# A six-stage transformer kernel on one core: DVE's program without engine loops, its waits on constants, and without three semaphore increments

## The reference

```
x = x + 0.5 * _L0_ffn_ref(_layernorm(x), ...)     # stage 0: 128 -> 64, relu over 16 inner units, 64 -> 128
x = x + _L0_attn_ref(_layernorm(x), ...)          # stage 1: window attention, 16 heads, LN on q and k
x = x + 0.5 * _L0_ffn_ref(_layernorm(x), ...)     # stage 2: as stage 0
x = x + 0.5 * _L1_ffn_ref(_layernorm(x), ...)     # stage 3: product keys
x = x + _L1_attn_ref(_layernorm(x), ...)          # stage 4: attention of the top 51 queries of each head
x = x + 0.5 * _L1_ffn_ref(_layernorm(x), ...)     # stage 5: as stage 3
```

```
s, i = jax.lax.top_k(sim, k)
all_scores = (sx[..., :, None] + sy[..., None, :]).reshape(b, n, h, k * k)
scores, pk = jax.lax.top_k(all_scores, k)
o = jnp.einsum('bnd,bnhkd->bnhk', inputs, w_down)
o = jax.nn.gelu(o, approximate=False) * jax.nn.softmax(scores, axis=-1)
return jnp.einsum('bnhk,bnhkd->bnd', o, w_up)
```

## Time and profile before

| | us |
|---|---|
| median of 3 runs (1404.76 to 1406.58) | 1404.99 |
| the profiled execution: time / span | 1402.47 / 1400.3 |
| busy: PE / DVE / ACT / POOL | 1151.0 / 1115.1 / 914.3 / 721.3 |
| stage 0 (its prep to 28.4; FFN to 94.9) | 94.9 |
| stages 1 / 2, with their preps | 217.0 / 69.4 |
| prep of stage 3; stage 3 to the last product-key result | 21.3; 381.9 |
| stage 4, with its prep | 212.0 |
| prep of stage 5; stage 5 | 21.5; 382.3 |
| bout_bc's DMA: issue to landing | 3.0 |

### The profile page before, as it was taken

One profiled execution on the slowest core, in us unless ns is written; L12 is line 12 of the kernel. 1 busy time (PEld: TensorE's weight loads), 2 busy tenths in 40 slices (PEclk: granted clock), 3 DMA queues, 4 the chain that ended last, 5 costly groups with the idle time before them and its releaser, 6 DMA issues.

```text
span 1400.3 us, 58159 instructions
## 1 busy us (share of the span) xinstructions
PE 1151.0 (82%) x22892; PEld 944.9 (67%) x22892; DVE 1115.1 (80%) x3996; ACT 914.3 (65%) x2135; POOL 721.3 (52%) x645
## 2 busy tenths in 40 slices
PE   1773898976758899999999769999568999999986
PEld 1562666655727788888888447777447888888886
DVE  4873888867879899989995468888598889998980
ACT  1772566647657778787785426666558787787871
POOL 3315444514037778777775410000157778787772
PEclk9886999988959999999999979999769999999998
DMA  6000000000002222222222000000012222222222
GB/s 160 17 0 1 1 0 0 0 2 0 1 0 48 47 45 53 52 45 45 45 45 63 1 1 1 0 0 1 0 22 54 49 45 45 45 60 45 45 62 77
DMA packets 27519, 42.91 MB, mean 31 GB/s; under 512 B 6960, under 2 KB 18480, under 8 KB 27440
## 3 DMA queue, kind: packets, MB, share of 16 engines
q1 hardware_dynamic: 27440, 41.82, 13.5%
HBM read 6.15 MB, written 2.10 MB: 6 GB/s over the span
## 4 chain that ended last, share of the span: by engine, by line
PE 42%; DVE 23%; ACT 11%; issue 11%; POOL 6%; DMA 3%; SPq 2%; DVEq 1%; POOLq 0%; ACTq 0%
PE bank L1763 11%; DVE work L909 5%; POOL work L346 5%; ACT work L1075 4%; DVE work L952 4%; PE bank L1745 4%; DMA rowsD<-work 3%; PE bank L1471 3%; ACT L1234 2%; PE bank L1647 2%; SPq L316 2%; DVE bank L934 2%; PE bank L1484 2%; PE bank L1629 2%; PE bank L1736 2%
## 5 line engine op out<-in xcount | busy, mean ns | idle before, releaser
L1763 PEld LDWEIGHTS bank<-rowsD,work 128*32 128x32 f32 x16384 | 359.5, 194 | 91.8 <-issue 91.2
L1763 PE MATMUL bank<-rowsD,work 128*32 128x32 f32 x16384 | 370.3, 275 | 56.4 <-DMA rowsD<-work 37.3
L421 POOL TENSOR_SCALAR work<-work 128x1024 f32<-128x1024 f32 x64 | 185.2, 2894 | 135.1 <-ACT work L1239 135.1
L408 POOL TENSOR_TENSOR work<-work 128x512 f32<-128x512 f32 x128 | 161.3, 1283 | 40.2 <-ACT work L1267 28.6
L1267 ACT ACTIVATE work<-bank 128x512 f32<-128x512 f32 x128 | 74.8, 610 | 152.0 <-PE bank L1763 148.8
L1239 ACT ACTIVATE work<-work 128x128 f32<-128x128 f32 x512 | 161.0, 404 | 4.1 <-DVE work L972 4.1
L1248 ACT ACTIVATE work<-work 128x128 f32<-128x128 f32 x512 | 160.2, 409 | 0.0
L423 POOL TENSOR_TENSOR work<-work 128x1024 f32<-128x1024 f32 x64 | 157.2, 2456 | 5.3
L952 DVE STREAM_TRANSPOSE work<-work 128x1024 f32<-128x1024 f32 x128 | 151.2, 1219 | 0.0
L453 POOL TENSOR_SCALAR xn<-x_sb,negmean,rstd 128x128 f32<-128x128 f32 x48 | 25.8, 539 | 207.9 <-DVE shift L562 179.6
L1774 PE MATMUL bank<-kout,work 128*128 128x128 f32 x1024 | 128.1, 278 | 3.0 <-POOL work L408 3.0
(11 more groups left out here) (193 smaller groups left out, 2315.7 us busy)
## 6 DMA issues: line engine op xcount, KB each, us to landing
rowsD<-work SPq DMA_DIRECT2D x256, 128.0 KB, 2.4
x_sb<-in_L_attn_x_dram SPq DMA_DIRECT2D x8, 256.0 KB, 4.7
out_dram<-x_sb SPq DMA_DIRECT2D x4, 512.0 KB, 5.3
headsel<-in_c_headsel_dram SPq DMA_DIRECT2D x1, 512.0 KB, 5.4
work<-in_L_ffn_key_in_dram SPq DMA_DIRECT2D x1, 512.0 KB, 8.0
kout<-in_L_ffn_key_out_dram SPq DMA_DIRECT2D x4, 128.0 KB, 4.3
work<-in_L_ffn_keys_dram SPq DMA_DIRECT2D x1, 256.0 KB, 2.9
wqkv<-in_L_attn_W_qkv_dram SPq DMA_DIRECT2D x1, 192.0 KB, 5.3
```

Of the source, the lines that this page charges most:

```text
L408: last = nc.gpsimd.tensor_tensor(cg[:, par, :].rearrange("p (j t) -> p j t", j=NCH)[:, :, half * 64:half * 64 + 64], csb[:, par, 512 * hal ...
L421: nc.gpsimd.tensor_scalar(wmask, both, 1.0 - 5e-7, None, ALU.is_ge).then_inc(s["wm"], 1)
L1763: last = nc.tensor.matmul(bank[2 + half][k * NK:(k + 1) * NK, :] .rearrange("p (j t c) -> p t c j", j=NCH, t=16)[:, t % 16, :, :], xrows[: ...
```

## The change

All of DVE's engine loops become Python loops, so the program holds every iteration with constant waits and addresses. The three `dve.sem_inc(s_go, 1)` are left out. Other engines keep their programs. Lines below L533 move up by one, those below L907 by two and those below L932 by three.

```diff
             def statistics(first, count, s, updated):
 
                 dve.wait_ge(s["x"], updated)
-                dve.sem_inc(s_go, 1)
                 for t in range(count):
...
                 if k == 0:
                     dve.wait_ge(s_x, 16 * NG)
-                    with dve.Fori(0, NT) as n:
+                    for n in range(0, NT):
                         nc.vector.bn_stats(stats[:, bass.ds(n, 1), :], x_sb[:, bass.ds(n, 1), :]).then_inc(s["stat"], 1)
...
-                    with dve.Fori(0, NG // 2 - 1) as i:
+                    for i in range(0, NG // 2 - 1):
                         sums(2 * i + 1, 1)
                         update(2 * i, 0)
...
-                with dve.Fori(0, NP_ // 2 - 2) as i:
+                for i in range(0, NP_ // 2 - 2):
                     sequence(2 * i + 1, 1)
                     sequence(2 * i + 2, 0)
...
                     dve.wait_ge(s["sim"], base + n + 1)
-                    dve.sem_inc(s_go, 1)
                     for c in range(2 * PH):
...
                     dve.wait_ge(s["cand"], base + n + 1)
-                    dve.sem_inc(s_go, 1)
                     for h in range(PH):
...
-                with dve.Fori(1, NPAIR - 1) as p:
+                for p in range(1, NPAIR - 1):
                     tile(2 * p, 0)
                     tile(2 * p + 1, 1)
```

## The result

The changed kernel took 1384.66 us (median of 4 runs, 1382.69 to 1385.71) against 1404.9 us before (median of 4, 1404.76 to 1406.58): ratio 0.9854, 95% interval 0.9841 to 0.9866. That is 1.5% less time, clear of the noise though smaller than 2%. The forecast was 1383.4 us. The profiled execution took 1384.7 us (span 1382.8) where that of before took 1402.47 (span 1400.3).

The account below looks back on a forecast made before the run. No engine's total decides: DVE alone paces stage 0's statistics, ACT leads the FFN, and a closed ring of waits paces stages 3 and 5. Terms summed to 21.6 us, taking 1404.99 to 1383.4; range 1375 to 1394.5.

Parts of the forecast that it names:

- the ring: Stages 3 and 5: DVE, SyncE's rowsD DMA, PE and ACT wait in a closed circle, 22.14 and 21.71 us a pair.
- (a): Stage 0's loop of 32 statistics: each goes from 0.492 to 0.197 us, saving 9.3 us (8.9 to 9.5).
- (b): Stage 0's FFN loop: DVE gains 0.5 us per pair of groups, but ACT leads; saving 0.7 us (0 to 1.9).
- the halving: Stage 0's FFN: of DVE's gain, 1.5 to 1.9 us, less than half was counted, 0.7 us, since ACT leads.
- (c): Increments of s_go, about 0.11 us each where DVE sets the time: 0.8 us in stage 2, 0.3 at stage ends.
- (d): Stage 3, inside the ring: 0.44 us a pair over 14 pairs, 6.2 us (3.5 to 9.1), plus 0.4 at its start.
- the piece set aside as plus or minus 0.2: L913 inside the ring, 0.60 to 0.86 us long: shifting it may give or take 0.2 us a pair, 2.8 a stage.
- (g): Longer program, DVE's listed instructions 1291 to 3986: at most 52 more instruction packets, hidden if fetched ahead, cost 0.
- (e): Stage 5, without statistics: 0.25 us a pair over 14 pairs, 3.5 us (1.4 to 6.3), plus 0.4 at its start.
- (f): Stages 1 and 4: DVE is on neither chain, so 0 (0 to 0.5, counted in the stage ends).
- fetches show: Rival: 21 to 52 new fetches each stall DVE 1.87 us inside the ring; 1423 us at the low end, chance 0.05.
- the two losses named there: Stage 3's lower bound, 0.25 us a pair: 0.15 us stay before L535, and L985 gains nothing.

Follow-up runs that it names:

- the product-key run: Kernel before with only DVE's product-key loop unrolled and the two increments of its front left out: 1397.44 us, ratio 0.9954.
- the statistics loop alone: Kernel before with one edit, stage 0's loop over 32 statistics unrolled: 1391.63 us, ratio 0.9909.
- either pad: Changed kernel plus one extra DVE reciprocal per product-key tile pair: in even tiles (inside the ring) 1387.43 us, in odd tiles (outside it) 1385.46 us.

## Why the prediction was right, and which terms were off

The forecast of 1383.4 us and its range held, and of the steps the largest two, the statistics loop and the ring, were right in mechanism. Several sizes were off, and partly cancelled.

- **(a) The statistics loop**, 9.3 us: 9.24 us measured from the first statistic to PE, in the changed kernel and alone. The price per instruction was exact; x landed 0.27 us sooner besides.
- **(b) Stage 0's FFN**, 0.7 us (0 to 1.9): 1.7 us measured. DVE's own gain, 0.5 us in a pair of groups, was sized rightly (11.16 to 10.64). The step that failed is the halving, "DVE can only give back the lag with which it ends behind ACT". A group went from 5.58 to 5.32 us. ACT's eight blocks, 0.66 us apart, need 5.3 us, so both engines were within 0.3 us of each other, and the chain by line named one of them.
- **(c) The increments**, 0.11 us each: 0.110 by the product-key run, 0.11 by the group of stage 0, and nothing for the one in front of L909. In stage 2, 0.8 us were forecast and 0.2 came: most groups fell by 0.11 us, but in one DVE now waits 0.46 us for ACT.
- **(d) Stage 3**, 0.44 us a pair: 0.31, stage and prep 4.6 us against 6.6. L978 to L909 gave 0.39 where 0.33 was forecast. The second part, 0.12 from L909 to L934, came to nothing, because L911 became longer in the odd tiles (0.63 to 0.78 us in the rows of one pair, median of all 0.64 to 0.77). That was the piece set aside as plus or minus 0.2. The rest is (g).
- **(e) Stage 5**, 0.25 us a pair: 0.19; by the medians of the pairs (21.73 to 21.46) it is 0.27. L978 to L909 gave 0.18 and L909 to L934 0.13, together 0.31, and SP to PE took 0.12 back, which is the fetches of (g).
- **(f) Stages 1 and 4**, 0: right as a mechanism. The +1.7 us of stage 1 is the granted clock, which the repeated run shows (217.3 us with nothing changed) and the line through all twelve traces. Stage 4's -0.9 was +0.7 in the repeated run.
- **(g) A longer program**, 0: this is the term that was wrong in kind. The instruction queue brought 23 packets more, within the 52 allowed for. DVE itself never stood still for a fetch: its only two issue idles after, 0.2 us each, at L682 and L735, were there before (L683, L736). But a fetch that falls into the transfer to rowsD delays it, and PE waits for that transfer in the ring. The rival "fetches show" looked for the cost on DVE and was off there; its path was the DMA. It cost 0.6 us in one pair of stage 3 (22.38 against 21.75) and 0.75 and 0.6 in two of stage 5 (22.21 and 22.06 against 21.45), 2.0 us together.

  Over the ring's eleven pairs per stage, the kernels with DVE's loop (before, the statistics loop alone) have no such fetch and no pair more than 0.3 us above the median. The seven runs with it unrolled and the transposes in their old place (six programs) have two or three such pairs each, 18 in all, and each of the 18 has a fetch 2.6 to 3.4 us behind the issue of its transfer. The sixteen from 3.2 us on cost 0.40 to 0.86 us, the four at 2.6 us (two of them not among the 18) 0.18 to 0.39. Fetches in the half microsecond before the issue, and at 1.9 and 4.4 us behind it, cost nothing. Where an edit shifts the fetches to other tiles the long pairs move with them: in stage 3 tile 23 in after and in its repetition, 9 with the increments back, 15 with either pad. No run moved a fetch and nothing else, but no pair speaks for another cause.

  The Trainium skill ("Runtime: NRT & Kernel Launch", Instruction fetch mechanics) calls straight-line fetch mostly hidden. For the engine that executes, the trace agrees (no issue idle at L907 or L534); for a transfer beside it, it doesn't.

Two slips in the recorded sums change nothing above. The upper ends of the terms add up to 29.0 us, not 29.2. And L913's 0.2 us a pair is in the upper bounds of (d) and (e) alone: the 0.25 us of (d) is used up by the two losses named there, and 14 x 0.12 for L934 alone is 1.7, not 1.4.

The 20.2 us of the medians against 17.5 of the traces is what one profiled execution can be off. Part of it is the clock. At 217.1, 216.0 and 218.8 us of stage 1, 43.0, 36.9 and 49.8 us lie at the lower level: 0.22 us of time for each (0.23 by all twelve traces). The Trainium skill ("TensorE: Matmul & The Clock Gate", Part 1: The HAM clock gate) says that the chip judges PE's activity on a rhythm that does not restart with the kernel, so that the moment of a change varies by run; the two stage-1 times of one program (218.8 and 217.3 us, at 49.8 and 43.2 us of the lower level) agree. The mean clock of the runs with the statistics loop alone is 0.936, that of before beside them 0.932, some 11 us less at the lower level, which at that rate would be 2.4 of the 3.5 us unaccounted for there. That is argued, not shown, and the remaining 1 us stays open. So does what stretches L911: it follows its position beside other engines' work, and no run isolated it.

## What to carry to other kernels

Draw the ring before counting instructions: the wait that comes back once per iteration shows which half of an engine's work has a price, and a pad of 0.2 us in either half tests it, if it is read in the iterations of the trace; the kernel's time is too noisy for it. Then ask first what can leave the ring. One step stood behind 4.3 us of work that it didn't need, with its inputs ready before that work began. Moving it gave 35 to 39 us, nearly twice what removing all of DVE's loop overhead gave, and made that removal worth 28 to 30 us instead of 20. The next bound came at once, PE's own work, so the gain was less than the 46 us that the ring alone promised. Where two engines are within 0.3 us of each other, the chain names one, and savings on the other may still count until it catches up.

## What the runs showed of the hardware

- A semaphore increment between a wait for a result of DVE itself and the next instruction costs DVE 0.11 us, in three places the same; behind a wait for PE, long met, it cost nothing (0.530 us with and without). A loop round of one instruction costs 0.295 us more than the instruction unrolled.
- With an 8 KB instruction packet that starts about 3.2 us behind the issue of a 4 x 128 KB transfer, PE's products come 0.4 to 0.9 us later, sixteen times of sixteen, although the packet is 0.3% of the queues' time in that stretch.
- The same pause of PE of 1.0 us went with under 4 us at 1.2 GHz in one execution, with 7 us in another execution of the same program, and with none in a third, of another program but with the same work in that stage. Between the first two, the stage of 217 us moved by 1.5 us.
